# Attention scores of two heads in two row halves of TensorE, with three score banks and one query bank

## What is computed

```python
h0 = relu(cnorm(conv(x, conv0_w, conv0_b, 5, 3)))     # channel norm after the first convolution, and so on
...
q = q.reshape(Bx, Tx, QPG, N_KV, D_HEAD).transpose(0, 2, 3, 1, 4)      # 16 heads of 64
k = k.reshape(Bx, Tx, 1, N_KV, D_HEAD).transpose(0, 2, 3, 1, 4)        # one key head
q = _rmsnorm(_rope(q), q_norm_w)
k = _rmsnorm(_rope(k), k_norm_w)
mask = (cols <= rows) & (rows - cols <= WINDOW)
scores = jnp.einsum('bqgtd,bqgsd->bqgts', q, k) * scale
scores = jnp.where(mask[None, None, None], scores, NEG)
attn = jax.nn.softmax(scores, axis=-1)
out = jnp.einsum('bqgts,bqgsd->bqgtd', attn, v)
...
return out @ wo.T
```

## Time and profile before

| what | us |
|---|---|
| time, median of 3 runs (2022.39 to 2023.54) | 2023.27 |
| the profiled execution, its own time | 2023.89 |
| its span, first to last instruction | 2021.9 |
| PE busy in the span | 1886.8 (93%) |
| DVE busy | 1499.7 (74%) |
| ACT busy | 1386.7 (69%) |
| POOL busy | 907.6 (45%) |

### The profile page before, as it was taken

One profiled execution on the slowest core, in us unless ns is written; L12 is line 12 of the kernel. 1 busy time (PEld: TensorE's weight loads), 2 busy tenths in 40 slices (PEclk: granted clock), 3 DMA queues, 4 the chain that ended last, 5 costly groups with the idle time before them and its releaser, 6 DMA issues.

```text
span 2021.9 us, 32941 instructions
## 1 busy us (share of the span) xinstructions
PE 1886.8 (93%) x9438; PEld 1353.6 (67%) x9509; DVE 1499.7 (74%) x3307; ACT 1386.7 (69%) x3881; POOL 907.6 (45%) x1545
## 2 busy tenths in 40 slices
PE   4999999999999959999968999999999999999998
PEld 2777778777777748877746666666666666665443
DVE  5778887887878755666548888887788777786765
ACT  1567677776777643444438888888888888887665
POOL 0122122222222200322368888888878888984200
PEclk9999999999999979999959999999999999999999
DMA  3211111111111000000000000000000000004554
GB/s 100 87 44 32 48 32 40 40 33 47 32 42 34 12 0 1 1 0 1 1 1 1 1 1 1 1 1 1 1 1 1 2 1 1 1 1 150 200 187 178
DMA packets 30509, 68.88 MB, mean 34 GB/s; under 512 B 14108, under 2 KB 14748, under 8 KB 28028
## 3 DMA queue, kind: packets, MB, share of 16 engines
q1 hardware_dynamic: 30332, 66.78, 10.3%
HBM read 45.12 MB, written 2.36 MB: 23 GB/s over the span
## 4 chain that ended last, share of the span: by engine, by line
PE 38%; POOL 8%; issue 8%; DVE 7%; ACT 3%; DMA 1%; DVEq 0%; POOLq 0%; ACTq 0%
PE ps L1169 6%; PE ps L65 3%; PE ps L67 3%; PE ps L66 3%; PE ps L1191 3%; PE ps L1743 3%; PE ps L1201 3%; PE ps L1180 2%; POOL atq L1527 2%; POOL atq L1534 2%; POOL apb L1541 2%; PE ps L1154 2%; PE ps L1166 1%; PE ps L1729 1%; PE ps L1730 1%
## 5 line engine op out<-in xcount | busy, mean ns | idle before, releaser
L1428 ACT ACTIVATE apb<-ps,amx 128x128 f32<-128x128 f32 x1024 | 361.1, 367 | 70.6 <-DVE amx L1294 69.3
L1541 POOL TENSOR_TENSOR apb<-apb,arc 128x512 f32<-128x512 f32 x256 | 267.7, 1046 | 69.3 <-DVE arc L1302 67.7
L1294 DVE TENSOR_REDUCE amx<-ps 128x4 f32<-128x512 f32 x256 | 176.0, 688 | 146.3 <-PE ps L1169 146.0
L1169 PE MATMUL ps<-akT,aqT 128*128 128x256 f32 x1024 | 264.9, 381 | 7.4 <-issue 3.5
L563 POOL TENSOR_TENSOR h0h<-h0h,const 128x1 fp32r<-128x1 f32 x256 | 46.0, 215 | 401.5 <-DVE h0l L462 401.5
L1169 PEld LDWEIGHTS ps<-akT,aqT 128*128 128x128 f32 x1024 | 198.1, 193 | 21.7
L1428 ACT ACTIVATION_READ_ACCUMULATOR apb<-ps,amx 128x1 f32 x1024 | 210.8, 206 | 0.0
L462 DVE SCALAR_TENSOR_TENSOR h0l<-ps,h0h 128x1024 fp32r<-128x1024 f32 x128 | 156.1, 1219 | 69.2 <-ACT h0h L380 69.2
L65 PE MATMUL ps<-h0h,w123h 128*128 128x512 f32 x512 | 203.4, 397 | 0.0
L66 PE MATMUL ps<-h0l,w123h 128*128 128x512 f32 x512 | 202.5, 396 | 0.0
L67 PE MATMUL ps<-h0h,w123l 128*128 128x512 f32 x512 | 202.4, 395 | 0.0
(11 more groups left out here) (312 smaller groups left out, 4938.8 us busy)
## 6 DMA issues: line engine op xcount, KB each, us to landing
h<-gates SPq DMA_DIRECT2D x8, 2048.0 KB, 7.8
atq<-gates SPq DMA_DIRECT2D x8, 2048.0 KB, 7.3
x0k<-x0h SPq DMA_DIRECT2D x128, 72.0 KB
x<-in_x SPq DMA_DIRECT2D x32, 192.0 KB, 2.6
x0k<-x0l SPq DMA_DIRECT2D x64, 72.0 KB
x0k<-x0h SPq DMA_DIRECT2D x64, 48.0 KB
out<-akT SPq DMA_DIRECT2D x16, 128.0 KB, 1.9
x0k<-x0l SPq DMA_DIRECT2D x32, 48.0 KB
```

The costliest lines, as they stand in the source:

```text
L1169: last = pe.matmul(bank[:, p * 2 * T:(p + 1) * 2 * T], qT[:, i % 2, 2 * k + p, :], kT[:, i // 4 % 2, i % 4, :, :].rearrange("p a s -> p (a ...
L1294: ve.tensor_reduce(mx[:, n % 4, :], ps[:, SB[n % 2], :].rearrange("p (h s) -> p h s", h=4), AX_X, ALU.max, negate=True).then_inc(S["mx"], 1)
L1428: last = ac.activation(pb[:, i % 2, head, :], ps[:, SB[n % 2], h * T:(h + 1) * T], ACT.Exp, bias=mx[:, k, h:h + 1], accum_out=sm[:, i % 2, ...
L1541: po.tensor_tensor(p, p, rc[:, i % 2, 4 * k:4 * k + 4].unsqueeze(2).to_broadcast([T, 4, T]), ALU.mult).then_inc(S["pn"], 1)
```

## The change

Scores are made for two parts at once, in even slots. `qT` is not changed; for each of four pairs of heads two matmuls are issued, one from rows 0 to 63 and one from rows 64 to 127, each of 128 columns, and each row half writes a bank of its own. The keys are held twice without zeros, so `kT` is half as wide, its memset goes, and `keep_k` is one instruction on 128 rows where it was two on 64. There are three score banks and one query bank: `scores(m)` waits for `exps` of part 2m - 2, and `project(m)` for `square(m - 1)`. `QT` moves to bank 4. The heads of a part are now 8h + a, 8h + a + 2 and so on (a the half), and `p_v` reads them as a block. `statv` becomes two f32r matmuls on a high and a low part of `gx`, which DVE splits in two new instructions (`split_gx`), placed after `low0(0, 0)`. The last group of the pooling is scheduled closer together (the four instructions of `weights` of a quad in one slot, quads in neighbouring slots; `pool`, `whiten`, `back` in neighbouring slots), `back` writes bank 5 there, and the waits at the start of the attention are fitted to that. The first expert banks follow the new numbers.

```diff
...
+        gxh, gxl = (sb(n, [GR, CHUNK], F32R) for n in ("gxh", "gxl"))
+        onesg = sb("onesg", [GR, GR], F32R)
...
                 def statv(i):
-                    pe.wait_ge(s_gx, i + 1)
-                    pe.matmul(ps[0:GR, XB, :], K["blkones"][0:GR, 0:GR], gx[:], start=True, stop=True
-                              ).then_inc(s_v, 1)
+                    pe.wait_ge(s_gxl, i + 1)
+                    pe.matmul(ps[0:GR, XB, :], onesg[:], gxh[:], start=True, stop=False)
+                    pe.matmul(ps[0:GR, XB, :], onesg[:], gxl[:], start=False, stop=True).then_inc(s_v, 1)
...
+                def split_gx(i):
+                    if i in halved:
+                        return
+                    halved.append(i)
+                    ve.wait_ge(s_gx, i + 1)
+                    if i >= 1:
+                        ve.wait_ge(s_v, i)
+                    high, low = split(ve, gxh[:], gxl[:], gx[:])
+                    high().then_inc(s_gxh, 1)
+                    ve.wait_ge(s_gxh, i + 1)
+                    low().then_inc(s_gxl, 1)
...
-                    (product, 0), (norm("1b"), 3), (low0(0, 0), 1), (split_next("1b"), 3), (split_sq("1a"), 2),
+                    (product, 0), (norm("1b"), 3), (low0(0, 0), 1), (split_gx, 0), (split_next("1b"), 3), (split_sq("1a"), 2),
...
-    normed = {g: full[g + 1] + 1 if g < LAST else full[g] + 19 for g in full}
+    normed = {g: full[g + 1] + 1 if g < LAST else full[g] + 13 for g in full}
...
-    at_pool = {full[g] + 7 + k if g < LAST else full[g] + 11 + 3 * k: i for i, (g, k) in home.items()}
+    at_pool = {full[g] + 7 + k if g < LAST else full[g] + 9 + k: i for i, (g, k) in home.items()}
...
-                slot = full[g] + 5 if g < LAST else full[g] + 5 if i == a else full[g] + 7 + 3 * (i - a) + max(n - 1, 0)
+                slot = full[g] + 5 if g < LAST else full[g] + 5 + i - a
...
-    SB, QB, QT, TB, OB, XB = (0, 1), (3, 4), 2, 5, 6, 7
+    SB, QB, QT, TB, OB, XB = (0, 1, 2), 3, 4, 5, 6, 7
...
-    kT = sb("akT", [2 * DH, 2, 4, 2, T])
+    kT = sb("akT", [2 * DH, 2, 4, T])
...
         def project(m):
             i, h = m // 2, m % 2
-            if i >= 1:
-                pe.wait_ge(S["sq"], m - 1)
+            if m >= 1:
+                pe.wait_ge(S["sq"], m)
...
-        def scores(n):
-            i, k = n // 4, n % 4
-            if n >= 2:
-                pe.wait_ge(S["ex"], n - 1)
-            if n % 16 == 0:
+        def scores(m):
+            i, h = m // 2, m % 2
+            banks = [ps[:, SB[n % 3], :] for n in (2 * m, 2 * m + 1)]
+            if m >= 1:
+                pe.wait_ge(S["ex"], 2 * m - 1)
+            if m % 8 == 0:
                 pe.wait_ge(S["kT"], i // 4 + 1)
-            pe.wait_ge(S["qT"], 2 * i + k // 2 + 1)
-            bank = ps[:, SB[n % 2], :]
-            pe.matmul(bank, identb[:], maskb[:].rearrange("p a s -> p (a s)"), start=True, stop=False,
-                      skip_group_check=True)
-            for p in range(2):
-                last = pe.matmul(bank[:, p * 2 * T:(p + 1) * 2 * T], qT[:, i % 2, 2 * k + p, :],
-                                 kT[:, i // 4 % 2, i % 4, :, :].rearrange("p a s -> p (a s)"), start=False,
-                                 stop=True, skip_group_check=True)
-            last.then_inc(S["s"], 1)
+            pe.wait_ge(S["qT"], m + 1)
+            for bank in banks:
+                pe.matmul(bank, identb[:], maskb[:].rearrange("p a s -> p (a s)"), start=True, stop=False,
+                          skip_group_check=True)
+            for p in range(4):
+                for a, bank in enumerate(banks):
+                    rows = slice(a * DH, (a + 1) * DH)
+                    last = pe.matmul(bank[:, p * T:(p + 1) * T], qT[rows, i % 2, 4 * h + p, :],
+                                     kT[rows, i // 4 % 2, i % 4, :], start=False, stop=True,
+                                     skip_group_check=True)
+                    if p == 3:
+                        last.then_inc(S["s"], 1)
...
-            if 0 <= u < PARTS:
-                scores(u)
+            if 0 <= u < PARTS and u % 2 == 0:
+                scores(u // 2)
             if u == min(at_pt):
-                pe.wait_ge(made["wx"], QUADS - 1)
+                pe.wait_ge(made["h4"], QUADS)
...
-            for a in range(2):
-                rows = slice(a * DH, (a + 1) * DH)
-                last = ac.activation(kT[rows, q % 2, :, a, :],
-                                     ps[rows, XB, :].rearrange("p (r s) -> p r s", r=4), ACT.Copy)
-            last.then_inc(S["kT"], 1)
+            ac.activation(kT[:, q % 2, :, :], ps[:, XB, :].rearrange("p (r s) -> p r s", r=4), ACT.Copy
+                          ).then_inc(S["kT"], 1)
...
```

64 lines of the change are left out of this document (34 added, 30 removed).

## The result

The changed kernel takes 1997.76 us (median of 4 runs, 1996.87 to 1999.48); the kernel before, run beside it, 2023.4. The ratio is 0.9874, 95% interval 0.9857 to 0.9891: 25.6 us or 1.3% faster. The sign was right; the time lies above the range of 1914 to 1992.

The account below looks back on a forecast made before the run. PE was taken to set the pace in convolutions and attention. Sums of blocks -11.5, passage into attention -8.5, scores -64 and passage into experts +1.5 gave -82.5 us, from 2023.9 to 1941 us; 8-in-10 range 1914 to 1992.

Parts of the forecast that it names:

- The sign: Whole kernel: the change was forecast to make it faster, with a chance of 84%.
- the range of 1914 to 1992: Whole kernel's time in us: the forecast's range of 8 in 10, around 1941 us.

Follow-up runs that it names:

- `halves_in_turn`: The changed kernel with the four score matmuls of rows 0 to 63 first, then the four of rows 64 to 127: 2048.5 us, ratio 1.0120.
- `before_scale_first`: The kernel before the change, with `scale_q` put ahead of the normalization on POOL: 1998.3 us, ratio 0.9875.
- `recip_first`: The changed kernel with DVE doing the reciprocal of the previous part ahead of the maximum of the current part in even slots: 1999.1 us, ratio 0.9885.
- `recip_keys`: The changed kernel with the reciprocal ahead of the maximum in even slots and POOL's sum of rotated keys one slot later: 1979.4 us, ratio 0.9787.
- `keys_later`: The changed kernel with `scale_q` ahead of the normalization on POOL and the sum of rotated keys one slot later: 1946.4 us, ratio 0.9621.

## What to carry to other kernels

Before an engine that is 96% busy is taken as the bound, follow its largest wait round the circle, through the place in the queue of each step and not only through the data it needs; a step that stands behind another's wait has that wait too. Then compute each such round against the period that is hoped for: one that ties with the old period leaves nothing to a faster engine. And where a circle runs through two steps of one engine that don't need each other, swap them before anything else; here that was worth more than the faster matmuls.

## What the hardware showed

- (Changed kernel and `halves_in_turn`.) Matmuls of 64 rows alternating between two row halves, fp32, 128 columns: 16 passes with their loads in 1.10 us; the same in turn, half after half, 1.64.
- A full fp32 step that follows one in array halves starts its own successor 0.05 to 0.06 us later than behind a full step (changed kernel against `before_scale_first`).
- Two idle stretches of PE, 0.54 and 1.75 us within 3 us, were followed in every second quad by some 3 us at a granted clock of 0.50, worth 1.5 us (`recip_first`); with 0.55 and 1.05 us it didn't happen in the steady quads (`recip_keys`). In `keys_later` the granted clock is 1.00 over the whole stretch from 1084 to 1762 us.
- A POOL multiplication of 128x512 that takes 1.04 us took 2.02 beside a DVE instruction of 1024 columns that lasted 1.36 (changed kernel, 1436.79).
